# Expert outputs weighted and scattered to token order, and a last stage that reads them in order and adds on TensorE

## The chip, the cores and the metric

One core of a Trainium2 chip. The metric is device time of the whole program in microseconds, median over runs.

## The reference, cut to what matters

```python
x = x + _layernorm(attn_ref(_layernorm(x), ...))      # x: (32, 512, 256) float32; a Mamba scan and a block of layers
h = _layernorm(x)                                     # no gain, no bias
weights = router(h)                                   # per token: softmax over its 2 best of 8 experts
caw = weights * (cumsum(weights > 0, axis=0) <= 2048) # an expert takes its first 2048 tokens
out = relu(tokens @ first_linear.T) @ second_linear.T # per expert: 256 -> 512 -> 256
final = zeros.at[index].add(out * vals)               # each token: weighted sum of its experts' rows
x = x + _layernorm(final)
```

There are 16384 tokens and 8 experts of 2048 slots. A token that finds its experts full gets rows of zeros.

## The kernel before

`build` runs three phases, each a block of its own in which all five engines have their own program, with semaphores between them.

`attention_phase` (L109 to 1165) goes over 32 sequences of 512 tokens. A scan of 32 steps per sequence (`scan`) carries three interleaved streams of other work: `pre` for the next sequence, `post` and `late` for those behind. Each is a generator that yields slot numbers (three slots per scan step), which fixes the order by hand on each engine. On SP, `load_rows` (L351 to 358) brings B and C rows for the step two ahead, 512 KiB each, into rings of two and four buffers. VectorE's drive (L960) reads the B rows. `late` writes x1 (the residual sum) to DRAM, routes the tokens, puts weights and slots aside in `w_all` and `idx_all`, and GpSimd scatters each normalised row of `tb` to its two slots in `expert_in` with eight indirect DMAs (L555). `expert_in` was cleared at the start by ScalarE's DMAs (L571).

`expert_phase` (L1168 to 1307) goes over 32 blocks of 512 slots, four to an expert. SP loads weights (L1213, 1215) and slots X (L1219), TensorE turns X, multiplies twice (L1246, 1256), ScalarE and VectorE share the relu, VectorE copies the output from PSUM to O (L1305), and ScalarE stores O in slot order to `expert_out`. X, XT, I and O have two buffers.

`combine_phase` (L1310 to 1470) goes over 32 sequences with G = 4 buffer sets. VectorE clears two row tiles and copies indices (L1433 to 1435), GpSimd gathers rows for 4 tiles and 2 choices with eight indirect DMAs (L1388), ScalarE multiplies the first choice by its weight (L1403), VectorE adds the second (L1444) and takes statistics (L1449, 1454), ScalarE computes the power with two table functions (L1410, 1412) and normalises (L1417), VectorE adds x1 (L1467), SP stores. `turns` writes each engine's parts out in order: a part `(back, part)` handles the sequence `back` places behind.

## Time and profile before

| what | value |
|---|---|
| median of 3 runs (lowest, highest) | 7221.53 us (7217.19, 7222.52) |
| the profiled execution: time, span | 7217.93 us, 7216.2 us |
| busy: TensorE, VectorE, ScalarE, GpSimd | 5483.0, 5886.2, 3552.3, 4301.8 us |
| DMA: packets, MB, mean GB/s | 492087, 1297.78, 180 |
[...]

Busy is the time in which an engine had an instruction at work. The profile is of one execution. Lines are those of the kernel before. TensorE's fp32 product of 512 columns is recorded as two records. [...]

### The profile page before, as it was taken

What the parts mean: (1) busy time and instruction counts of PE and PEld (TensorE: products, weight loads), DVE (VectorE), ACT (ScalarE), POOL (GpSimd) and SP (SyncE); (2) the same over time, 40 slices, a digit from 0 to 9 for tenths busy, and PEclk for the clock granted to TensorE, in tenths of its full rate; (3) what the DMA queues carried; (4) which work ended last, traced back from release to release, by engine and by line L of the source; (5) the groups of instructions that cost most, each with busy time, mean ns of one, the idle gap of its engine ahead of it and who ended that gap; (6) DMA issues with size and microseconds to landing.
All of it is one profiled execution on the core that took longest, in us unless ns stands there. A gap on an engine that the chain in (4) does not pass through costs nothing. (4 is left out here: it accounts for less than half of the span.)

```text
span 7216.2 us, 70913 instructions
## 1 busy us (share of the span) xinstructions
PE 5483.0 (76%) x16640; PEld 2999.0 (42%) x16640; DVE 5886.2 (82%) x7907; ACT 3552.3 (49%) x5338; POOL 4301.8 (60%) x2865
## 2 busy tenths in 40 slices
PE   4788778888887888878788888888887888599700
PEld 1344444444444444444444444444444444466400
DVE  5999999999999999989999999999999998211255
ACT  3555555555555555555555555555555554111156
POOL 3666666666666666666666666666666666200176
PEclk8899898889999988898988889989989988699855
DMA  7656556655655555555555555555555555022253
GB/s 262 215 193 197 192 198 200 202 195 195 203 203 188 194 194 191 195 189 194 193 190 189 193 191 200 193 192 189 196 194 184 187 188 194 11 91 87 78 160 94
DMA packets 492087, 1297.78 MB, mean 180 GB/s; under 512 B 59311, under 2 KB 216625, under 8 KB 490561
## 3 DMA queue, kind: packets, MB, share of 16 engines
q1 hardware_dynamic: 440960, 1219.82, 50.7%
q10 hardware_dynamic: 26048, 38.95, 1.6%
q0 software_dynamic: 24576, 33.72, 1.5%
q8 instruction: 143, 2.34, 0.1%
q14 instruction: 360, 2.94, 0.1%
HBM read 1206.19 MB, written 119.54 MB: 184 GB/s over the span
## 5 line engine op out<-in xcount | busy, mean ns | idle before, releaser
L480 POOL TENSOR_TENSOR st<-st,C_rows 128x1024 f32<-128x1024 f32 x1024 | 2470.6, 2415 | 1155.7 <-DVE st L988 1154.3
L787 PE MATMUL y<-st,ident 128*128 128x512 f32 x4096 | 2163.0, 663 | 472.2 <-POOL st L480 426.5
L988 DVE TENSOR_TENSOR_SCAN st<-dA,drive 128x1024 f32<-128x1024 f32 x1024 | 2338.7, 2284 | 177.2 <-ACT dA L642 85.2
L642 ACT ACTIVATE dA<-delta,a_neg 128x511 f32<-128x511 f32 x2048 | 1382.3, 713 | 2155.2 <-DVE st L988 2146.7
L787 PEld LDWEIGHTS y<-st,ident 128*128 128x128 f32 x4096 | 830.3, 212 | 1520.0 <-issue 899.1
L960 DVE TENSOR_TENSOR drive<-du,B_rows 128x1024 f32<-128x1024 f32 x1024 | 1259.5, 1230 | 101.3 <-DVE du L955 18.2
L761 PE MATMUL pre_bank<-e_abs,in_w 128*128 128x512 f32 x1024 | 601.6, 718 | 178.2 <-DVE u L926 161.9
L1388 POOL DMA_INDIRECT rows<-expert_out,idx_c x256 | 266.3, 1040 | 621.5 <-DVE idx_c L1435 551.4
L555 POOL DMA_INDIRECT expert_in<-tb,idx x256 | 259.8, 1015 | 367.0 <-DVE idx_all L1163 306.0
L741 PE MATMUL post_bank<-d_w,gT 128*128 128x256 f32 x2048 | 467.0, 385 | 12.4 <-issue 11.6
L741 PEld LDWEIGHTS post_bank<-d_w,gT 128*128 128x128 f32 x2048 | 394.3, 193 | 119.9 <-issue 67.7
L761 PEld LDWEIGHTS pre_bank<-e_abs,in_w 128*128 128x128 f32 x1024 | 211.4, 219 | 445.6 <-issue 209.7
L926 DVE SCALAR_TENSOR_TENSOR u<-pre_bank,conv_w,u 128x511 f32<-128x511 f32 (+2 forms) x384 | 285.3, 743 | 22.6 <-ACT u L598 13.6
L642 ACT ACT_TABLE_LOAD x217 | 278.4, 1283 | 3.8
L741 PE MATMUL post_bank<-q_w,F 128*128 128x256 f32 x512 | 184.3, 538 | 121.2 <-ACT F L664 121.2
L937 DVE TENSOR_SCALAR rest<-e_abs 128x1024 f32<-128x1024 f32 x64 | 233.6, 3650 | 25.5 <-ACT e_abs L623 19.4
L858 PE MATMUL post_bank<-F,d_w 128*128 128x512 f32 x512 | 236.0, 604 | 20.6 <-ACT F L695 20.5
L468 POOL TENSOR_TENSOR rest<-e_abs,rest 128x1024 f32<-128x1024 f32 x64 | 179.2, 2800 | 107.9 <-DVE rest L937 107.9
L1246 PE MATMUL bank<-XT,w 128*128 128x512 f32 x512 | 229.9, 603 | 10.1 <-ACT XT L1273 10.1
L1305 DVE COPY O<-bank 128x512 f32<-128x512 f32 x64 | 41.2, 686 | 234.5 <-PE bank L1256 234.5
L1256 PE MATMUL bank<-w,I 128*128 128x256 f32 x1024 | 228.6, 381 | 3.3 <-issue 3.3
L858 PE MATMUL pre_bank<-F,d_w 128*128 128x512 f32 x512 | 230.2, 592 | 0.0
(190 smaller groups left out, 8027.8 us busy)
## 6 DMA issues: line engine op xcount, KB each, us to landing
B_rows<-bc_rows SPq DMA_DIRECT2D x1024, 512.0 KB
C_rows<-bc_rows SPq DMA_DIRECT2D x1024, 512.0 KB
xin<-in_x SPq DMA_DIRECT2D x32, 512.0 KB, 7.3
expert_in<-gT ACTq DMA_DIRECT2D x8, 2048.0 KB, 27.2
xn_rows<-xin SPq DMA_DIRECT2D x32, 512.0 KB, 6.2
h<-xn_rows SPq DMA_DIRECT2D x32, 512.0 KB, 6.5
x_res<-in_x SPq DMA_DIRECT2D x32, 512.0 KB, 3.6
x_rows<-x_res SPq DMA_DIRECT2D x32, 512.0 KB, 3.2
```

Of the source, the lines that this page charges most:

```text
L480: pool.tensor_tensor(tile[:, :, :], tile[:, :, :], bc[1][k % ROWS[1]][:, :, :], ALU.mult)\
L555: pool.indirect_dma_start(out=xe_dram, out_offset=bass.IndirectOffsetOnAxis(ap=idx[:, tile, choice:choice + 1], axis=0), in_=tb[:, tile, : ...
L642: return act.activation(dA[k % 2][:, j, 1:L], delta[par][:, c, 1:L], ACT.Exp, scale=a_neg[:, c, n:n + 1])
L741: last = pe.matmul(banks[tile // 2][:, (tile % 2) * D:(tile % 2 + 1) * D], srcT[:, c, tile * P:(tile + 1) * P], w[:, c, :], start=c == 0, ...
L761: last = pe.matmul(RB[m % 2][:, :], in_w[:, c, m * P:(m + 1) * P], xT[:, c, :], start=c == 0, stop=c == KD - 1)
L787: last = pe.matmul(Y[:, :], ident[:, :], st[k % RING][:, j, :], start=pair == 0 and j == 0, stop=pair == CU - 1 and j == 1)
L858: last = pe.matmul(FB[j % 4][:, :], d1_w[:, c, j * P:(j + 1) * P], F[:, c, :], start=c == 0, stop=c == KD - 1)
L926: dve.scalar_tensor_tensor(late, RB[c % 2][:, 0:L - 1 - j], conv_w[:, c, 2 - j:3 - j], late, ALU.mult, ALU.add).then_inc(pre_dve.did(f"con ...
L937: dve.tensor_scalar(rest[:, :, :], e_abs[:, c:c + 2, :], 1.0, 1.0, ALU.add, ALU.subtract)\
L960: dve.tensor_tensor(DR[:, :, :], DU[:, :].unsqueeze(1).to_broadcast([P, 2, L]), bc[0][k % ROWS[0]][:, :, :], ALU.mult).then_inc(scan_in.di ...
L988: dve.tensor_tensor_scan(st[k % RING][:, :, :].rearrange("p a l -> p (a l)"), dA[k % 2][:, :, :].rearrange("p a l -> p (a l)"), DR[:, :, : ...
L1388: pool.indirect_dma_start(out=rows[n][c][:, tile, :], out_offset=None, in_=ye_dram, in_offset=bass.IndirectOffsetOnAxis(ap=idx_c[n][:, til ...
```

## The change

Rows of `expert_in` become 264 floats wide: behind the 256 features stand the token's two weights, its two expert numbers and its own number, all kept in `tb_wide`; `w_all` and `idx_all` go. In the expert stage VectorE finds out which choice of the token this expert is, and from it the slot's weight and a destination row, `choice * 16384 + token`. The output is multiplied by the weight as it leaves PSUM, and GpSimd scatters it with four indirect DMAs per block into `rank_rows`, which holds 2 x 16384 rows in token order. Unused slots have an index out of bounds and are not written. `rank_rows` is cleared by one 1 MiB DMA per sequence on SP during attention. One sequence of x1 is loaded behind each block's X into `x1_all`, which holds all 32 (128 KiB per partition), four tokens to a partition. The last stage loads both choices' rows of a sequence in one DMA, adds them in PSUM by four products with the identity, takes statistics on VectorE from PSUM, the power on GpSimd, normalises on ScalarE in PSUM, adds x1 on VectorE and stores from `x1_all`.

The diff, cut; of the last stage only the new lines are shown:

```diff
@@ -84,24 +84,27 @@
     xn_v = [rows.rearrange("(t p) d -> p t d", p=P) for rows in xn_dram]
     x1_dram = nc.dram_tensor("x1_rows", (S, L, D), F32, kind="Internal").ap()
     x1_v = x1_dram.rearrange("s (t p) d -> s p t d", p=P)
-    xe_dram = nc.dram_tensor("expert_in", (NSLOT, D), F32, kind="Internal").ap()
-    ye_dram = nc.dram_tensor("expert_out", (NSLOT, D), F32, kind="Internal").ap()
-    xe_zero_v = xe_dram.rearrange("(a p r) d -> a p (r d)", p=P, r=16)
+    x1_wide_v = x1_dram.rearrange("s (p t) d -> s p t d", p=P)
+    out_wide_v = t["out"].rearrange("s (p t) d -> s p t d", p=P)
+    DW = D + 8
+    xe_dram = nc.dram_tensor("expert_in", (NSLOT, DW), F32, kind="Internal").ap()
+    xe_zero_v = xe_dram.rearrange("n d -> (n d)").rearrange("(a p r) -> a p r", p=P, r=12 * D)
     xe_v = xe_dram.rearrange("(n t p) d -> n p t d", t=TB, p=P)
-    ye_v = ye_dram.rearrange("(n t p) d -> n p t d", t=TB, p=P)
+    yr_dram = nc.dram_tensor("rank_rows", (2 * NTOK, D), F32, kind="Internal").ap()
+    yr_zero_v = yr_dram.rearrange("(s p r) d -> s p (r d)", s=S, p=P)
+    yr_v = yr_dram.rearrange("(c s p t) d -> s p c t d", c=2, s=S, p=P)
     with ExitStack() as whole:
         def sem(name):
             return whole.enter_context(nc.semaphore(name))
-        idx_all = whole.enter_context(nc.sbuf_tensor("idx_all", [P, S * TT, 2], U32))
-        w_all = whole.enter_context(nc.sbuf_tensor("w_all", [P, S * TT, 2], F32))
         ident = whole.enter_context(nc.sbuf_tensor("ident", [P, P], F32))
         ones = whole.enter_context(nc.sbuf_tensor("ones", [P, P], F32))
-        eps5 = whole.enter_context(nc.sbuf_tensor("eps5", [P, 1], F32))
         attention_phase(nc, t, dict(locals()), sem)
+        x1_all = whole.enter_context(nc.sbuf_tensor("x1_all", [P, S, TT, D], F32))
+        x1_loaded = sem("x1_loaded")
         expert_phase(nc, t, dict(locals()), sem)
         combine_phase(nc, t, dict(locals()), sem)
...
@@ -195,7 +197,13 @@
         F = sb("F", [P, KD, L])
         gT = sb("gT", [P, KF, L])
         h = sb("h", [P, TT, D])
-        tb = sb("tb", [P, TT, D])
+        tb_wide = sb("tb", [P, TT, DW])
+        tb = tb_wide[:, :, 0:D]
+        wts = tb_wide[:, :, D:D + 2]
+        top_f = tb_wide[:, :, D + 2:D + 4]
+        token = tb_wide[:, :, D + 4]
...
@@ -371,6 +379,10 @@
                 sp.wait_ge(*post_dve.at("h_sum", b - 2))
...
                 sp.dma_start(xn_v[par], xin[:, :, :]).then_inc(xn_stored, 16)
+                yield 44
+                zero_row = zeros[:, :].unsqueeze(1).to_broadcast([P, 2 * TT * D // zeros.shape[1], zeros.shape[1]])
+                sp.dma_start(yr_zero_v[b].rearrange("p (a r) -> p a r", r=zeros.shape[1]), zero_row)\
+                    .then_inc(rank_rows_zeroed, 16)
                 yield 50
                 sp.wait_ge(*pre_act.at("xd", b))
                 sp.dma_start(bc_dram[par], xd[R:NX, :]).then_inc(xd_stored, 16)
...
@@ -421,7 +434,10 @@
+            pool.memset(zeros[:, :], 0.0).then_inc(consts, 1)
+            pool.iota(next_token[:, :], pattern=[[P, TT]], base=-int(FAR), channel_multiplier=1,
+                      allow_small_or_imprecise_dtypes=True).then_inc(consts, 1)
+            pool.memset(tb_wide[:, :, D:DW], 0.0).then_inc(consts, 1)
...
@@ -554,7 +570,7 @@
                     tile, choice = divmod(n, 2)
                     pool.indirect_dma_start(
                         out=xe_dram, out_offset=bass.IndirectOffsetOnAxis(ap=idx[:, tile, choice:choice + 1], axis=0),
-                        in_=tb[:, tile, :], in_offset=None, bounds_check=NSLOT - 1, oob_is_err=False)\
+                        in_=tb_wide[:, tile, :], in_offset=None, bounds_check=NSLOT - 1, oob_is_err=False)\
...
@@ -568,8 +584,8 @@
                     act.dma_start(dst, src).then_inc(post_weights_in, 16)
             act.wait_ge(zero_tile, 1)
             for a in range(xe_zero_v.shape[0]):
-                act.dma_start(xe_zero_v[a], gT_flat).then_inc(zeroed, 16)
-            act.wait_ge(consts, 13)
+                act.dma_start(xe_zero_v[a], gT_flat[:, 0:xe_zero_v.shape[2]]).then_inc(zeroed, 16)
+            act.wait_ge(consts, 15)
             act.wait_ge(pre_weights_in, 16 * len(PRE_IN))
...
@@ -1132,7 +1148,10 @@
                 dve.wait_ge(*late_dve.at("oh1_pos", b))
                 dve.tensor_tensor(asg[:, :, :], oh[0][:, :, :], oh[1][:, :, :], ALU.add)\
                     .then_inc(late_dve.did("asg"), 1)
-                dve.tensor_copy(w_all[:, bass.ds(b * TT, TT), :], wts[:, :, :]).then_inc(late_dve.did("w_all"), 1)
+                dve.tensor_copy(token, next_token[:, :]).then_inc(late_dve.did("token"), 1)
+                dve.wait_ge(*late_dve.at("token", b))
+                dve.tensor_scalar(next_token[:, :], next_token[:, :], float(L), None, ALU.add)\
+                    .then_inc(late_dve.did("next_token"), 1)
...
@@ -1159,8 +1178,6 @@
                         .then_inc(late_dve.did(f"slot{i}"), 1)
                 dve.wait_ge(*late_dve.at("slot1", b))
                 dve.tensor_scalar(idx[:, :, :], slot_f[:, :, :], FAR, None, ALU.add).then_inc(late_dve.did("idx"), 1)
-                dve.wait_ge(*late_dve.at("idx", b))
-                dve.tensor_copy(idx_all[:, bass.ds(b * TT, TT), :], idx[:, :, :]).then_inc(late_dve.did("idx_all"), 1)
             all_sequences(dve, pre, scan, post, late)
...
@@ -1194,10 +1221,22 @@
+        e_meta = Steps(sem("e_meta"), [f"{name}{n}" for n in range(NB) for name in
+                                       (("mine", "w_mine", "w_slot", "dest", "dest_i")
+                                        + (("expert",) if n % QB == QB - 1 else ()))])
+        expert_set = sem("expert_set")
+        carried_pool_e = sem("carried_pool_e")
+        XL = S // (NE // 2 * NB)
+        assert XL * (NE // 2) * NB == S
+        def before_meta(n, i):
+            return e_meta.at(f"dest{n - 2}", i) if n >= 2 else e_meta.at(f"dest{NB + n - 2}", i - 1)
...
@@ -1216,7 +1255,13 @@
                             .then_inc(w_loaded[e], 16)
                     sp.wait_ge(*before(e_turn, n, 2, i))
...
+                    sp.wait_ge(*before_meta(n, i))
...
                     sp.dma_start(X[n % 2][:, :, :], xe_v[i * NB + n]).then_inc(slots_loaded[n % 2], 16)
+                    for part in range(XL):
+                        at = (i * NB + n) * XL + part
+                        sp.dma_start(x1_all[:, bass.ds(at, 1), :, :], x1_wide_v[bass.ds(at, 1)]
+                                     .rearrange("s p t d -> p s t d")).then_inc(x1_loaded, 16)
         @block.tensor
         def _(pe):
...
@@ -1282,15 +1325,56 @@
                             .then_inc(e_relu_act.did(n * KE // 2 + m // 2), 1)
                     if n + 1 < NB:
                         copy_turned(n + 1)
-                    act.wait_ge(*e_out.at(n, i))
-                    act.dma_start(ye_v[i * NB + n], O[n % 2][:, :, :]).then_inc(stored[n % 2], 16)
-            for half in range(2):
-                act.wait_ge(stored[half], 16 * (NE // 2) * (NB // 2) + 16)
+        @block.gpsimd
+        def _(pool):
+            e_sent.credit(pool)
+            with pool.Fori(0, NE // 2) as i:
+                for n in range(NB):
+                    pool.wait_ge(*e_out.at(n, i))
...
+                    pool.wait_ge(*e_meta.at(f"dest_i{n}", i))
...
+                    for tile in range(TB):
+                        pool.indirect_dma_start(
+                            out=yr_dram, in_=O[n % 2][:, tile, :], in_offset=None,
+                            out_offset=bass.IndirectOffsetOnAxis(ap=dest_i[n % 2][:, tile:tile + 1], axis=0),
+                            bounds_check=2 * NTOK - 1, oob_is_err=False).then_inc(stored, 16)
+                    pool.wait_ge(stored, 16 * TB * NB * i + 16 * TB * (n + 1))
+                    pool.sem_inc(e_sent.did(n), 1)
         @block.vector
         def _(dve):
-            for steps in (e_relu_dve, e_out):
+            for steps in (e_relu_dve, e_out, e_meta):
                 steps.credit(dve)
+            dve.memset(expert[:, :], 0.0).then_inc(expert_set, 1)
+            dve.wait_ge(expert_set, 1)
+            def slots_meta(n, i):
+                meta = X[n % 2]
+                dve.wait_ge(slots_loaded[n % 2], 16 * (NB // 2) * i + 16 * (n // 2 + 1))
...
+                if n % QB == 0:
+                    dve.wait_ge(*(e_meta.at(f"expert{n - 1}", i) if n else e_meta.at(f"expert{NB - 1}", i - 1)))
+                dve.tensor_scalar(mine[:, :, :], meta[:, :, D + 2:D + 4], expert[:, 0:1], None, ALU.is_equal)\
+                    .then_inc(e_meta.did(f"mine{n}"), 1)
+                dve.wait_ge(*e_meta.at(f"mine{n}", i))
+                dve.tensor_tensor(w_mine[:, :, :], mine[:, :, :], meta[:, :, D:D + 2], ALU.mult)\
+                    .then_inc(e_meta.did(f"w_mine{n}"), 1)
+                dve.wait_ge(*e_meta.at(f"w_mine{n}", i))
+                dve.tensor_reduce(w_slot[:, :], w_mine[:, :, :], AX_X, ALU.add)\
+                    .then_inc(e_meta.did(f"w_slot{n}"), 1)
+                dve.scalar_tensor_tensor(dest[:, :], mine[:, :, 1], float(NTOK), meta[:, :, D + 4],
+                                         ALU.mult, ALU.add).then_inc(e_meta.did(f"dest{n}"), 1)
+                dve.wait_ge(*e_meta.at(f"dest{n}", i))
+                dve.wait_ge(*before(e_sent, n, 2, i))
+                dve.tensor_scalar(dest_i[n % 2][:, :], dest[:, :], FAR, None, ALU.add)\
+                    .then_inc(e_meta.did(f"dest_i{n}"), 1)
+                if n % QB == QB - 1:
+                    dve.tensor_scalar(expert[:, :], expert[:, :], 1.0, None, ALU.add)\
+                        .then_inc(e_meta.did(f"expert{n}"), 1)
             with dve.Fori(0, NE // 2) as i:
...
@@ -1298,47 +1382,45 @@
                         dve.wait_ge(*e_mm1.at(n * KE + m, i))
                         dve.tensor_scalar(I[n % 2][:, m, :], MB[m][:, 0:BLK], 0.0, None, ALU.max)\
                             .then_inc(e_relu_dve.did(n * KE // 2 + m // 2), 1)
+                    slots_meta(n, i)
                     dve.wait_ge(*e_mm2.at(n, i))
-                    dve.wait_ge(stored[n % 2], 16 * (NB // 2) * i + 16 * (n // 2 + 1))
-                    for tile in range(0, TB, 2):
-                        last = dve.tensor_copy(O[n % 2][:, tile:tile + 2, :],
-                                               OB[tile // 2][:, :].rearrange("p (a d) -> p a d", a=2))
+                    dve.wait_ge(*e_meta.at(f"w_slot{n}", i))
+                    for tile in range(TB):
+                        last = dve.tensor_scalar(O[n % 2][:, tile, :],
+                                                 OB[tile // 2][:, (tile % 2) * D:(tile % 2 + 1) * D],
+                                                 w_slot[:, tile:tile + 1], None, ALU.mult)
                     last.then_inc(e_out.did(n), 1)
 def combine_phase(nc, t, env, sem):
...
@@ -1360,114 +1442,101 @@
+            sp.wait_ge(x1_loaded, 16 * S)
...
+                sp.wait_ge(*c_sum.at(n, i - 1))
+                sp.dma_start(rows[n][:, :, :, :], yr_v[G * i + n]).then_inc(rows_loaded[n], 16)
+                sp.dma_start(out_wide_v[bass.ds(G * i + n, 1)].rearrange("s p t d -> p s t d"),
+                             x1_all[:, bass.ds(G * i + n, 1), :, :]).then_inc(out_stored, 16)
+            sp.wait_ge(out_stored, 16 * S)
+        @block.tensor
+        def _(pe):
+            c_sum.credit(pe)
+            def add(n, i):
+                pe.wait_ge(rows_loaded[n], 16 * (i + 1))
+                pe.wait_ge(*c_out.at(n, i - 1))
+                for half in range(TT // 2):
+                    for c in range(2):
+                        last = pe.matmul(total[n][:, 2 * half:2 * half + 2, :].rearrange("p t d -> p (t d)"), ident[:, :],
+                                         rows[n][:, c, 2 * half:2 * half + 2, :].rearrange("p t d -> p (t d)"),
+                                         start=c == 0, stop=c == 1)
+                last.then_inc(c_sum.did(n), 1)
+            turns(pe, ((0, add),))
+        @block.vector
+        def _(dve):
+            for steps in (c_stats, c_out):
+                steps.credit(dve)
+            dve.wait_ge(x1_loaded, 16 * S)
+            def stats(n, i):
+                dve.wait_ge(*c_sum.at(n, i))
+                for tile in range(TT):
+                    last = dve.bn_stats(stat[n][:, tile, :], total[n][:, tile, :])
+                last.then_inc(c_stats.did(f"stats{n}"), 1)
+                dve.wait_ge(*c_stats.at(f"stats{n}", i))
...
+                for tile in range(TT):
+                    last = dve.bn_aggr(mv[n][:, tile, :], stat[n][:, tile, :])
+                last.then_inc(c_stats.did(f"aggr{n}"), 1)
+            def add(n, i):
+                dve.wait_ge(*c_normed.at(n, i))
+                x1 = x1_all[:, bass.ds(G * i + n, 1), :, :].rearrange("p s t d -> p (s t d)")
+                dve.tensor_tensor(x1, total[n][:, :, :].rearrange("p t d -> p (t d)"), x1, ALU.add)\
+                    .then_inc(c_out.did(n), 1)
+            turns(dve, ((2, add), (0, stats)))
+            c_shift.credit(pool)
+            pool.memset(minus_half[:, :], -0.5).then_inc(c_const, 1)
+            pool.wait_ge(c_const, 1)
+            def scale_and_shift(n, i):
+                pool.wait_ge(*c_stats.at(f"aggr{n}", i))
...
+                pool.wait_ge(*c_normed.at(n, i - 1))
...
+                pool.tensor_scalar(shift[n][:, :], mv[n][:, :, 0], -1.0, None, ALU.mult).then_inc(c_shift.did(f"m{n}"), 1)
+                pool.tensor_scalar(r[n][:, :], mv[n][:, :, 1], LN_EPS, None, ALU.add).then_inc(c_shift.did(f"v{n}"), 1)
+                pool.wait_ge(*c_shift.at(f"v{n}", i))
+                pool.tensor_tensor(r[n][:, :], r[n][:, :], minus_half[:, :], ALU.pow).then_inc(c_shift.did(f"r{n}"), 1)
+                pool.wait_ge(*c_shift.at(f"r{n}", i))
+                pool.tensor_tensor(shift[n][:, :], shift[n][:, :], r[n][:, :], ALU.mult)\
+                    .then_inc(c_shift.did(f"shift{n}"), 1)
+            turns(pool, ((0, scale_and_shift),))
+            c_normed.credit(act)
+                act.wait_ge(*c_shift.at(f"shift{n}", i))
+                for tile in range(TT):
+                    last = act.activation(total[n][:, tile, :], total[n][:, tile, :], ACT.Identity,
+            turns(act, ((0, normalise),))
```

## Rows read from the trace of the kernel before

**Rows 1.** Stretches of the span: start:end, us, busy time (instructions) per engine, clock, DMA share, GB/s.

```profile
0.00:6311.88 6311.88, 5001.22 (x14848) 2677.77 (x14848) 5590.25 (x7203) 3263.09 (x4826) 4035.53 (x2609) 0.89 0.57 191
6311.88:6819.79 507.91, 481.81 (x1792) 321.26 (x1792) 85.48 (x128) 72.57 (x128) 0.00 (x0) 0.98 0.25 83
6819.79:7216.20 396.41, 0.00 (x0) 0.00 (x0) 210.42 (x576) 216.67 (x384) 266.30 (x256) 0.50 0.42 127
```

**Rows 2.** Groups of the combine stage: count | busy us, mean ns | idle before, releaser.

```profile
L1388 POOL DMA_INDIRECT rows<-expert_out,idx_c x256 | 266.3, 1040 | 621.5 <-DVE idx_c L1435 551.4 <-issue 70.1
...
L1444 DVE SCALAR_TENSOR_TENSOR rows<-rows,w_c,rows 128x256 f32<-128x256 f32 x128 | 53.4, 480 | 18.6 <-ACT rows L1403 17.5 <-issue 1.0
L1449 DVE BATCH_NORM_STATS2 c_stat<-rows 128x6 f32<-128x256 f32 x128 | 45.0, 414 | 16.6 <-remote 9.1 <-issue 5.3 <-DVE rows L1444 1.3
...
L1467 DVE TENSOR_TENSOR x<-x,rows 128x1024 f32<-128x1024 f32 x32 | 39.3, 1228 | 110.7 <-ACT rows L1417 89.7 <-issue 21.0
```

**Rows 3.** Timeline at the combine's start: start us, us, engine, instruction, [idle before].

```profile
6819.79 1.48 SPq L1369 DMA_DIRECT2D x<-x_rows  x3
...
6829.76 0.99 POOL L1388 DMA_INDIRECT rows<-expert_out,idx_c  x1 [0.30 <-issue]
```

**Rows 4.** Timeline of the program's start, ScalarE's clearing DMAs.

```profile
28.22 5.46 ACTq L571 DMA_DIRECT2D expert_in<-gT  x8
```

**Rows 5.** Timeline around slot 44 of one sequence, SP's queue and VectorE.

```profile
2991.68 0.34 SPq L357 DMA_DIRECT2D C_rows<-bc_rows  x1
2999.16 0.32 SPq L357 DMA_DIRECT2D B_rows<-bc_rows  x1
...
3007.63 1.23 DVE L960 TENSOR_TENSOR drive<-du,B_rows 128x1024 f32<-128x1024 f32 x1
```

**Rows 6.** The 32 loads of X (L1219, 512 KiB), from issue to landing.

```profile
DMA to landing us min/median/max: 3.7/3.9/6.4
```

**Rows 7.** Single microseconds of attention: TensorE busy (count), granted clock, DMA share, GB/s.

```profile
3047.00:3048.00 1.00, 0.00 (x0) 1.00 1.02 369
3048.00:3049.00 1.00, 0.00 (x0) 0.61 1.01 336
...
3054.00:3055.00 1.00, 1.00 (x2) 0.50 0.00 0
...
3056.00:3057.00 1.00, 1.00 (x7) 1.00 1.04 373
```

**Rows 8.** Timeline of the last expert block.

```profile
6799.61 6.60 PE L1246 MATMUL bank<-XT,w 128*128 128x512 f32 x15
...
6807.04 7.15 PE L1256 MATMUL bank<-w,I 128*128 128x256 f32 x32 [0.83 <-issue]
6814.23 1.29 DVE L1305 COPY O<-bank 128x512 f32<-128x512 f32 x2 [7.28 <-PE bank L1256]
6815.75 0.38 ACTq L1286 DMA_DIRECT2D expert_out<-O  x1
```

**Rows 9.** Timeline of one layer norm at the end of the attention stage.

```profile
6271.95 0.38 DVE L911 BATCH_NORM_AGGREGATE mv_late<-stat_late 128x2 f32<-128x6 f32 x4
...
6274.50 2.07 ACT L580 ACTIVATE tb<-tb,shift_late,r_late 128x256 f32<-128x256 f32 x4 [25.92 <-POOL shift_late L457]
```

**Rows 10.** Timeline of the border from attention to the experts.

```profile
6307.42 0.97 POOL L555 DMA_INDIRECT expert_in<-tb,idx  x1 [0.31 <-issue]
6311.88 0.40 SPq L1213 DMA_DIRECT2D w<-in_e_w  x1
...
6318.94 1.96 PE L1231 MATMUL bank<-ident,X 128*128 128x128 f32 x8 [23.08 <-DMA X<-expert_in]
```

**Rows 11.** Timeline: fp32 products of 512 columns at either clock.

```profile
45.10 6.77 PE L761 MATMUL pre_bank<-e_abs,in_w 128*128 128x512 f32 x8 [1.16 <-ACT e_abs L592]
...
3002.64 1.96 PE L787 MATMUL y<-st,ident 128*128 128x512 f32 x4
```

**Rows 12.** Timeline: the last add of the program.

```profile
7211.21 1.23 DVE L1467 TENSOR_TENSOR x<-x,rows 128x1024 f32<-128x1024 f32 x1 [2.14 <-ACT rows L1417]
```

158 lines of the change are left out of this document (50 added, 108 removed).

## The prediction

> **What bounds the kernel now.** I read the stretches first, then the groups of the last stage, the order of time around each border, and last the clock. The program is three stages one behind the other [rows 1]: attention and routing to 6311.88 us, the experts for 507.91 us, the combine for 396.41 us. In the first, VectorE is busy 5590 of 6312 us and is the limit. In the second, TensorE is busy 482 of 508 us at clock 0.98. In the third TensorE does nothing and the DMA share is 0.42; look there at the GpSimd row: 256 gathers [rows 2], one issued every 0.99 + 0.30 = 1.30 us [rows 3]. Eight for each sequence are 10.4 us, times 32 sequences 333 us of the 396; the rest is the fill, the drain and waits for the cleared buffers. ScalarE (two table loads a sequence) and VectorE lie beside it. So the combine is set by GpSimd's issuing, 12.4 us a sequence, and that is what the change removes.
>
> **The sum's base.** The profiled execution took 7217.9 us (span 7216.2), 3.6 us under the median of the runs shown, 7221.5; I work against 7217.9 and predict with no correction. Stages one and two and the combine are summed separately, and the new combine replaces 396.4 us.
>
> **Attention.** The two small copies per sequence (`w_all`, `idx_all`) go and two small ones (`token`, `next_token`) come, on VectorE both: nil. Scattered rows grow from 1024 to 1056 bytes, with the same eight issues: nil. SP now waits for GpSimd's constants before its first load of x; these are a handful of short fills done while SP issues weight loads: nil. ScalarE issues 11 instead of 8 clearing DMAs ahead of its first activation, on which the start hangs: eight took 5.46 us [rows 4], so three more are 2.0 us; rows are a quarter shorter, bounds 0 and 2.0, I take 1.4. New on SP's queue is one 1 MiB clearing write per sequence, at slot 44 of `pre`, which is behind the C load issued at 2991.68 and before the B load issued at 2999.16 in this sequence [rows 5]. The queue is to do 1.5 MiB in that 7.5 us gap. Behind it waits the B load, used by the drive at 3007.63, 8.5 us after its issue, where a 512 KiB load lands in 3.9 us [rows 6]. That leaves 4.6 us of cover, and the write moves at about 373 GB/s [rows 7] in 2.8 us. So nil; bounds 0 and 1 us per sequence (32 us), taken 0 because both covers would have to go.
>
> **Experts.** The path is TensorE: from the first product of a block's first layer at 6799.61 to the end of its second layer at 6814.19 lie 14.6 us, and it is busy all through [rows 8]. The X load waits also for VectorE's `dest` of the block two back, about half a block later than now; there remain more than 10 us until its transposes, against a landing of 3.9 us at the median and 6.4 at most [rows 6]. The 512 KiB load of x1 goes behind it in SP's queue. VectorE gets five or six tiny operations (four aggregates together cost 0.38 [rows 9]), under 2 us, between the second relu and the end of the second product, where it idled 7.28 us [rows 8]. The output becomes four scaled copies of 256 columns in place of two of 512. The nearest rows are the 1.29 us of now and four scalar_tensor_tensor at 480 ns [rows 2], 1.9 us at most; TensorE needs the banks one first product (7 us) later. GpSimd gets four scatters (5.2 us) and the wait for their landing, about 9 us for a block, and the buffer is wanted two blocks later. Nothing of this is on the path except behind the last block. There, before, 4.0 us lie between ScalarE's store and the first load of the combine [rows 3, 8]. After: 0.4 us more for the output, 0.2 us, four issues at 1.30, and then what lay between the end of the last scatter of the attention stage and the first load of the experts, 6311.88 - 6308.39 = 3.5 us [rows 10]. That is 9.3 us less 0.5 that both have, so 4.8 us are added (bounds 3 and 7). Where all this idle time is gone, an expert block pays at most about 2 us, 64 us in all; the cover is several times the cost, so I take 0.
>
> Before the combine that makes +6.2 us.
>
> **The new combine.** Per sequence: one 1 MiB load, four fp32 products with the identity (both choices summed in PSUM), bn_stats, GpSimd's power, ScalarE's normalise, one add, one 512 KiB store. It clears nothing, gathers nothing and loads no tables, and x1 lies in SBUF already. Throughput first: VectorE 1.41 + 0.38 + 1.23 = 3.0 us [rows 2, 9], GpSimd 2.0, ScalarE 2.1, 1.5 MiB at 373 GB/s 4.2 us, TensorE 8 records. Eight records took 6.77 us at the lower clock; four took 1.96 at the higher, so eight about 3.7 [rows 11].
>
> But the order of issue makes a ring. On SP `store(n-3)` stands before `load(n)`, so load n is issued only when the add of n-3 is done. On VectorE the add of n stands behind the statistics of n+1. From sum n+1 to the end of the add of n: statistics 1.41 + 0.15 + 0.38 = 1.95 (SBUF prices; PSUM could be up to 0.2 more), add 1.25, hops 0.1: 3.3 us. Sum n's own way to its add (statistics 1.95, GpSimd's four steps until ScalarE starts 2.17, normalise 2.07 [rows 9]: 6.2 us) is shorter than that, as long as the period is above 4.3. From there to sum n+3: hop 0.1, store and load, hop 0.1, products. For store and load I use two rows. Two weight loads and X, 1.5 MiB in one burst, took from 6311.88 to 6318.94, 7.06 us [rows 10], and one 512 KiB load alone takes 3.9 [rows 6]. So 3.16 us is for 1 MiB (332 GB/s) and 2.3 us is fixed. The new transfers have pieces of 4 KiB, as the B and C loads, in whose busy microseconds 369 and 373 GB/s stand [rows 7]: 4.2 + 2.3 = 6.5 us. So sum n+3 lies 3.3 + 6.7 + products after sum n+1, and the period T is half of 10.0 + products: 6.85 us at the higher clock, 8.4 at the lower.
>
> The products' clock: the granted clock was still 1.00 in the idle microsecond from 3047, fell to 0.61 in the next, was 0.50 in the microsecond from 3054, the last of nearly four busy ones, and 1.00 from 3056 [rows 7]. A burst of 3.7 us in a period of 7 leaves gaps of over 3 us; a burst of 6.8 leaves 1.6. I expect bursts of both kinds in turn, mean 5.25 us, T = 7.6.
>
> Fill: load 0 lands at 5.1 us, sum 0 at 12.0 (1.2 GHz), sum 1 at 17.3, add 0 done at 20.6, sum 3 at 32.6. Then 28 periods of 7.6, 213 us, then sum 31's way to its add, 6.2 + 1.3, and from the last add to the span's end 3.8 [rows 12]: 256.7 us. The sum is 7217.9 - 396.4 + 6.2 + 256.7 = **7084 us**.
>
> [...]
>
> **The rivals.** [...] (b) The ring doesn't bind, and transfers set the pace, because the landing time overlaps better than I think: T = 5.3, combine about 192, **7020 us**. For it: 4.2 us is the transfer time and three loads are in flight. Against it: the written order on SP and VectorE. (c) The covers in the first two stages are thinner, 1 us per sequence or block in one of them and 1 to 2 in the other: 7084 + 32 to 96, about **7140 us**. For it: VectorE is 89% busy in attention, so any stall there counts fully. (d) Slower than before: the clearing write holds the B loads back. It costs something once it takes over 8.3 us (3.7 of gap left by the C load, 4.6 of cover), and makes the kernel slower when each of 32 sequences stalls for over 4.2 us. At 5 us that is **7244 us**; the write would have to run at 79 GB/s, where the row shows 373. (e) The change doesn't do what it says: the combine stays at 12 us a sequence since something else as long as the gathers stands behind them: about 7215. Nothing in rows 2 is that long, since ScalarE's two table loads go too.
>
> **How the numbers follow.** Forecast 0.50 (7061 to 7109, T from 6.85 to 8.4); (a) 0.13; (b) 0.20; (c) 0.12; (d) 0.03; (e) 0.02. The prediction is 7084. The range reaches down to (b), 7020, and up to a part of (c), 7125, and leaves out about half of (c), (d), (e) and the faster end of (b). A measurement of this kernel can tell some 0.2% (14 us) from no change, and all of the forecast, (a), (b) and (c) lie beyond that: faster 0.95, same 0.02, slower 0.03.
>
> **What would show it.** The combine should be 235 to 282 us with sums 7 to 8.5 us apart, and TensorE waiting for the loaded rows, each load issued right after an add three back. VectorE should wait for the sums before its statistics. If the sums lie 5 us apart, (b). [...] The expert stage should be 508 + 5 us, the attention stage 6312 + 1.4; more there is (c) or (d), seen as VectorE's drive waiting for B_rows. A combine whose busy records of statistics or normalise are much longer from PSUM than from SBUF would make my 3.3 us wrong.

## The result and the profile after

| | before | after |
|---|---|---|
| device time, median (lowest to highest) | 7221.15 us (7217.19 to 7222.52, 4 runs) | 7121.35 us (7114.18 to 7126.48, 4 runs) |
| ratio | | 0.9862, interval 0.9845 to 0.9879 |
| profiled execution, time and span | 7217.9, 7216.2 us | 7119.3, 7117.5 us |
| attention and routing | 6311.88 us | 6339.18 us, +27.3 (forecast +1.4) |
| experts | 507.91 us | 506.73 us, -1.2 (forecast +4.8) |
| combine | 396.41 us | 271.59 us, -124.8 (forecast -139.7) |

The change takes 99.8 us off the median; the forecast was 137 (7221 to 7084). It is faster, by 1.4% and clear of its interval, and inside the range given, 7020 to 7125, near its upper end. By the profiles it is 98.7 us, and the three stage lines of the table add up to that. This is the view of stretches for the kernel after, as [rows 1]: start:end, us, then busy time (instructions) of PE, PEld, DVE, ACT and POOL, granted clock, DMA share, GB/s.

```profile
0.00:6339.18 6339.18, 5002.93 (x14848) 2691.31 (x14848) 5598.24 (x7204) 3263.38 (x4826) 4050.88 (x2611) 0.89 0.58 196
6339.18:6845.91 506.73, 480.12 (x1792) 320.56 (x1792) 120.47 (x360) 72.59 (x128) 124.86 (x129) 0.98 0.35 117
6845.91:7117.50 271.59, 153.62 (x256) 61.34 (x256) 95.91 (x288) 60.98 (x128) 54.68 (x128) 0.75 0.53 185
```

GpSimd's 266.30 us of gathers in the combine have become 54.68 us, and its 128 scatters stand in the expert stage, where it was at 0.00 before. No engine is busy for even 60% of the new combine. From the page of the kernel after, a group (count, busy us, mean ns, idle before with its releaser), and two DMA lines (count, KB each, us to landing):

```profile
L1472 PE MATMUL total<-rows,ident 128*128 128x512 f32 x256 | 153.6, 763 | 118.4 <-DMA rows<-rank_rows 118.2
...
rank_rows<-zeros SPq DMA_DIRECT2D x32, 1024.0 KB, 7.8
rows<-rank_rows SPq DMA_DIRECT2D x32, 1024.0 KB, 6.7
```

The 118.2 us in the first line is what the combine now waits for: loads. They land in 6.7 us at the median; they are issued late. One round in time order (start us, us, engine, instruction, idle before with its releaser; consecutive instructions of the same kind are drawn together):

```profile
6889.59 9.60 PE L1472 MATMUL total<-rows,ident 128*128 128x512 f32 x16 [6.71 <-DMA rows<-rank_rows]
...
6895.74 1.42 DVE L1489 BATCH_NORM_STATS2 c_stat<-total 128x6 f32<-128x256 f32 x4 [8.74 <-PE total L1472]
...
6897.61 1.19 DVE L1501 TENSOR_TENSOR x_all<-total,x_all 128x1024 f32 x1
...
6899.03 0.36 SPq L1456 DMA_DIRECT2D out<-x_all  x1
6899.23 1.42 DVE L1489 BATCH_NORM_STATS2 c_stat<-total 128x6 f32<-128x256 f32 x4 [0.43 <-PE total L1472]
6899.65 0.38 SPq L1451 DMA_DIRECT2D rows<-rank_rows  x1
...
6905.40 8.03 PE L1472 MATMUL total<-rows,ident 128*128 128x512 f32 x11 [6.21 <-DMA rows<-rank_rows]
...
6912.18 1.09 DVE L1489 BATCH_NORM_STATS2 c_stat<-total 128x6 f32<-128x256 f32 x3 [8.85 <-PE total L1472]
```

Read it as a ring. The sum that starts at 6889.59 frees VectorE's statistics at 6895.74; behind them in VectorE's order stands the add of the sequence before, done at 6898.80; it frees SP's store and, behind that, the next load, issued at 6899.65; its rows start TensorE at 6905.40. The sums come in pairs, 16.4 us apart (6895.74 to 6912.18). From load 3 at 6866.09 to load 31 at 7094.28 are 228.2 us for 28 periods, T = 8.15.

Single microseconds of that round (same columns as the stretches):

```profile
6887.00:6888.00 1.00, 0.00 (x0) 0.00 (x0) 0.01 (x1) 0.77 (x2) 0.20 (x1) 0.83 0.95 377
6890.00:6891.00 1.00, 1.00 (x2) 0.42 (x2) 0.00 (x0) 0.00 (x0) 0.00 (x0) 0.50 0.65 152
6894.00:6895.00 1.00, 1.00 (x3) 0.53 (x2) 0.00 (x0) 0.00 (x0) 0.00 (x0) 0.76 0.22 90
6896.00:6897.00 1.00, 1.00 (x4) 0.50 (x3) 1.00 (x4) 0.00 (x0) 0.00 (x0) 1.00 0.00 0
```

The first sum of the pair starts after 6.7 us of idleness, by the end of which the clock is 0.50. It takes 6.2 us (6889.59 to 6895.74), and the clock comes back in the last of it: 0.76 in the microsecond from 6894, 1.00 in the one from 6895. The second follows directly at clock 1.00 and takes 3.4 us. Over the stage the first sums of the 14 pairs from 6874.13 on took 5.2 to 6.8 us, 6.05 in the mean, and their starts lie 16.15 us apart in the mean. Each of the 14 starts at clock 0.50. The second sum of a pair has its rows already, or waits 1.2 us for them at the most, and takes 3.4 to 3.7 us.

The start of the program, where [rows 4] had eight DMAs in 5.46 us:

```profile
28.02 11.66 ACTq L587 DMA_DIRECT2D expert_in<-gT  x11
```

Eleven took 11.66 us: 6.2 more, where the forecast had 1.4 with an upper bound of 2.0.

The rest of attention's loss is in its loop. From the 336.69 us at which one store of `bc_rows` is issued to the last such of the loop, 5878.31, before took 5541.6 us; after (342.96 to 5909.27) took 5566.3: +24.7. The start had put +6.3 ahead of that, and the last stretch gives 3.7 back. The groups of the loop's window, 336 to 5900 us (count, busy us, mean ns, idle before), of the kernel before:

```profile
L555 POOL DMA_INDIRECT expert_in<-tb,idx x232 | 235.7, 1016 | 321.6 <-DVE idx_all L1163 266.4 <-issue 55.2
L1054 DVE TENSOR_SCALAR gcol<-post_bank,rg 128x2 f32<-128x2 f32 x30 | 6.6, 219 | 29.4 <-POOL rg L447 29.4
```

The same groups of the kernel after:

```profile
L571 POOL DMA_INDIRECT expert_in<-tb,idx x224 | 239.8, 1070 | 313.9 <-DVE idx L1180 252.0 <-issue 61.9
L1070 DVE TENSOR_SCALAR gcol<-post_bank,rg 128x2 f32<-128x2 f32 x29 | 6.3, 218 | 47.3 <-POOL rg L463 47.3
```

A scatter costs 54 ns more in the mean, and VectorE waits 18 us longer for GpSimd before `gcol`. One sequence shows which scatter it is, and nearly all others are like it. The timeline of the kernel before:

```profile
3000.34 0.17 DVE L1161 TENSOR_SCALAR idx<-slot_f 128x8 uint32<-128x8 f32 x1
...
3000.64 0.17 DVE L1163 COPY idx_all<-idx 128x8 uint32 x1
...
3002.82 0.98 POOL L555 DMA_INDIRECT expert_in<-tb,idx  x1 [0.30 <-issue]
3003.05 0.68 DVE L955 TENSOR_TENSOR du<-delta,u 128x512 f32<-128x512 f32 x1
...
3012.04 0.22 DVE L1054 TENSOR_SCALAR gcol<-post_bank,rg 128x2 f32<-128x2 f32 x1 [0.81 <-POOL rg L447]
```

The same place in the kernel after:

```profile
3017.79 0.17 DVE L1180 TENSOR_SCALAR idx<-slot_f 128x8 uint32<-128x8 f32 x1
...
3020.18 0.68 DVE L971 TENSOR_TENSOR du<-delta,u 128x512 f32<-128x512 f32 x1
...
3020.27 1.44 POOL L571 DMA_INDIRECT expert_in<-tb,idx  x1 [0.30 <-issue]
...
3029.95 0.22 DVE L1070 TENSOR_SCALAR gcol<-post_bank,rg 128x2 f32<-128x2 f32 x1 [1.58 <-POOL rg L463]
```

With the 0.17 us copy gone, VectorE reaches `du` 0.32 us sooner after `idx` (2.39 us against 2.71). Before, the second scatter started 0.23 us ahead of `du` and took 0.98 us; after, it starts 0.09 us behind `du` and takes 1.44. So it is in 28 of the loop's 29 sequences (in the other the second scatter comes later and is short in both kernels): before, the second scatter starts ahead of `du` in 27 and takes 0.97 or 0.98 us, and in the one where it starts 0.06 behind it takes 1.46; after, it starts 0.08 to 0.36 us behind `du` in each and takes 1.44 down to 1.17, so that it always ends some 1.52 us after `du` began. `gcol` waits for GpSimd's power, and comes 12.16 us after `idx` instead of 11.70: 0.46 us a sequence, some 14 us of the loop's 24.7.

In the expert stage, this is a loop's edge in the timeline of the kernel before:

```profile
6446.08 0.38 ACTq L1286 DMA_DIRECT2D expert_out<-O  x1
6447.05 1.07 ACT L1273 COPY XT<-bank 128x512 f32<-128x512 f32 x2 [11.80 <-issue]
...
6448.25 8.20 PE L1246 MATMUL bank<-XT,w 128*128 128x512 f32 x15 [3.08 <-ACT XT L1273]
```

And one in the kernel after:

```profile
6472.24 1.07 ACT L1316 COPY XT<-bank 128x512 f32<-128x512 f32 x2 [10.06 <-PE bank L1276]
...
6473.45 7.13 PE L1291 MATMUL bank<-XT,w 128*128 128x512 f32 x16 [1.34 <-ACT XT L1316]
```

Before, ScalarE had to issue the store of `expert_out` (and so wait for VectorE's output) ahead of the copy that TensorE waits for. With the store gone, TensorE waits 1.34 instead of 3.08 us. There are three such edges (3.08, 2.86 and 2.84 us before, 1.3 each after), which is 4.8 us. At this one the next sixteen records also took 8.63 us before and 7.13 after; at the other two they took 7.13 before already. This is read from the timelines; no run puts the store back. From the first transpose to the last product the stage took 488.8 us instead of 495.3.

### The profile page after: what moved, and what is told of

Same layout as the page of the kernel before. It is cut to its first block and busy times, and to the rows that moved or that the text cites. A ratio compares the mean times of both kernels' runs of the same rounds, so it can differ in the third digit from the quotient of the medians.

```text
span 7117.5 us, 71413 instructions
## 1 busy us (share of the span) xinstructions
PE 5636.7 (79%) x16896; PEld 3073.2 (43%) x16896; DVE 5814.6 (82%) x7852; ACT 3397.0 (48%) x5082; POOL 4230.4 (59%) x2868
## 5 line engine op out<-in xcount | busy, mean ns | idle before, releaser
L1339 POOL DMA_INDIRECT rank_rows<-O,dest_i x128 | 124.8, 975 | 382.1 <-issue 382.1
L1472 PE MATMUL total<-rows,ident 128*128 128x512 f32 x256 | 153.6, 763 | 118.4 <-DMA rows<-rank_rows 118.2
L1291 PE MATMUL bank<-XT,w 128*128 128x512 f32 x512 | 228.2, 599 | 5.3 <-ACT XT L1316 5.3
```

## The experiments

The attention stage ends with the first weight load of the experts; "border" below is its time (before 6311.88, after 6339.18). Each ratio is to the kernel before on the same chip. Chips differed: before had medians of 7191.9 us beside the first four, 7237.3 beside the next four and 7197.3 beside the last four. The gather stage took 396.4 us in the profile of the kernel before, but 373.2 and 375.4 us in the profiles of two variants that don't touch it (experiments three and ten), on other chips; why is not known. There the change is worth less: experiment two is the changed kernel with one write moved, and its ratio is 0.9904, 69 us, where the changed kernel itself had 0.9862. Where kernels stand beside each other I therefore go by the borders and the length of the combine.

**Is the clearing write the cause in attention?** First without it. The last stage reads x twice in place of the scattered rows.

```diff
-                yield 44
-                sp.dma_start(yr_zero_v[b]..., zero_row).then_inc(rank_rows_zeroed, 16)
 ...
-                sp.dma_start(rows[n][:, :, :, :], yr_v[G * i + n])
+                sp.dma_start(rows[n][:, :, :, :], x_rows.unsqueeze(1).to_broadcast([P, 2, TT, D]))
```

> The changed kernel without the 1 MiB clearing write per sequence; rank_rows is not cleared, and the last stage loads rows of x twice in its place (same transfer size, other data). Question: the attention stage of the changed kernel ends 27.3 us later than before, 6.2 of it at the start and 21 us gathered over 32 sequences. Theory A (the clearing write in flight beside the scatters and the B and C loads costs it): the first expert load comes 17 to 24 us earlier than 6339.2, the whole time is about 7101, and the idle time before VectorE's gcol (47 us against 27 before) falls back. Rival B (the wider rows of tb and the token copies cost it): the border stays within 5 us of 6339, the time at 7121.

Ratio 0.9879 (0.9864 to 0.9894), median 7107.1 us; the profiled execution, with a span of 7112.7, is the slowest of the four. Its border is at 6349.42, 10 us later than with the write, and the loop takes 5572.3 us. The loss isn't the clearing's. The added 10 us were expected by no theory. Some 4 of them are spread: the four profiles of experiments five to eight, whose attention stage is that of the changed kernel, have borders from 6338.73 to 6343.06. The rest is not explained.

**The write in another place of the same sequence.**

```diff
-                yield 44
 ...
+                yield 70
```

The three lines of the write move with it, behind the store of `bc_rows` at slot 50.

> The changed kernel with the clearing write at slot 70 of pre in place of 44, behind the last scatter (slot 53). Theory A1 (it costs because it runs beside the scatters, which GpSimd issues more slowly, and G's power waits behind them): the border between attention and experts comes 12 to 21 us earlier than 6339.2, time 7100 to 7109. A2 (1 MiB more per sequence costs wherever it stands): within 5 us of 6339, time 7116 to 7126. B (wide rows): no change either.

0.9904 (0.9889 to 0.9919), median 7122.9 us; the border is at 6340.40 and the loop takes 5566.3 us, as after. The place is of no account either.

**The write alone, in the kernel before**, with the tile of zeros that it reads and SP's wait for it.

```diff
 ...
+                sp.dma_start(yr_zero_v[b]..., zero_row).then_inc(rank_rows_zeroed, 16)
```

> The kernel before with the clearing write alone (1 MiB per sequence at slot 44 into a DRAM tensor that nobody reads). Theory A: 17 to 24 us slower than before, 7238 to 7245, all of it ahead of the expert stage. B: within 5 us of before, 7216 to 7226.

1.0001 (0.9992 to 1.001). Border 6315.42, which is 3.5 us later, scatters 1017 ns in the mean, the wait ahead of `gcol` 29.9 us in all. So 32 MiB of clearing beside the attention stage cost nothing clear of the noise, and the forecast's zero held.

**The eleven clearings of expert_in spread over the first scan**, so that nothing waits for their issue.

```diff
-            for a in range(xe_zero_v.shape[0]):
-                act.dma_start(xe_zero_v[a], ...).then_inc(zeroed, 16)
 ...
+                    if isinstance(b, int) and b == 0 and k < xe_zero_v.shape[0]:
+                        act.dma_start(xe_zero_v[k], ...).then_inc(zeroed, 16)
```

> The changed kernel with the 11 clearing DMAs of expert_in issued one by one in the first 11 steps of the first scan on ScalarE, and not ahead of its first activation. If ScalarE's issuing (11.7 us here, 5.5 before) stands on the path of the start, the whole program shifts by 10 to 12 us: 7109 to 7111. If the first loads of x or weights end later than I think, 0 to 5 us.

0.9921 (0.9906 to 0.9936), and the border went the wrong way, to 6356.70. The first store of `bc_rows` is 11 us earlier (64.73 against 75.57), but the one that stood at 342.96 is at 357.97. VectorE's waits between 70 and 350 us (us in total, times, longest), first with the clearings spread:

```profile
DVE drive L976 <- DMA B_rows<-bc_rows: 29.3, 10, 5.9
```

The same wait in the kernel after:

```profile
DVE drive L976 <- DMA B_rows<-bc_rows: 0.7, 1, 0.7
```

The 16.5 MiB of clearing now pass beside the first scan's loads, where VectorE is the limit, and the waits for those loads grow by 29 us, against the 11 us gained. It was expected 10 to 12 us faster than the kernel after; the border is 17.5 us later.

**The order on SP.** The load of n ahead of the store of n-3: the load of n now stands behind the add of n-4 in place of n-3, so the ring through the add holds one period more.

```diff
-            turns(sp, ((3, store), (0, load)))
+            turns(sp, ((0, load), (3, store)))
```

> The changed kernel with SP's two parts in the other order, load(n) ahead of store(n-3), so that a load is issued behind the add of four sequences back in place of three. Ring theory (period 8.15 us set by order of issue: half of 3.1 us from the first sum of a pair to an add, 6.6 to the landed rows, 6.5 for products at the lower clock): the ring now holds three periods, T = 16.3/3 = 5.4 us, or 4.7 if the clock stays up; the combine falls from 271.6 to 175 to 200 us, time 7025 to 7050. Rival (the transfers set the pace, 1.5 MiB in 8.15 us): no change, 7115 to 7126.

0.9725 (0.9709 to 0.9742), 7039.6 us. The combine takes 189.97 us, and from load 4 at 6868.99 to load 31 at 7015.60 T = 5.43 (the expectation of the last experiment has it as 5.24). View of stretches, as above:

```profile
6848.83:7038.80 189.97, 136.08 (x256) 54.58 (x256) 96.06 (x288) 60.89 (x128) 54.50 (x128) 0.84 0.75 265
```

This settles the ring: same instructions, same bytes, 82 us less.

**The order on VectorE.** The add of n-1 ahead of the statistics of n.

```diff
-            turns(dve, ((2, add), (0, stats)))
+            turns(dve, ((1, add), (0, stats)))
```

> The changed kernel with VectorE's add one place behind in place of two, so that the add of n no longer stands behind the statistics of n+1. Ring theory: the ring becomes 7.4 (statistics, power, normalise, add) + 6.6 + products over three periods: 17.5 to 20.5 us, T = 5.9 to 6.8, the combine 210 to 235 us, time 7060 to 7085. Rival (transfers set the pace): no change.

0.9817 (0.98 to 0.9833); the combine takes 255.2 us, a miss of 20 us at the least. The timeline shows what took the ring's place:

```profile
6881.59 1.22 DVE L1501 TENSOR_TENSOR x_all<-total,x_all 128x1024 f32<-128x1024 f32 x1 [4.21 <-ACT total L1535]
...
6882.73 1.42 DVE L1489 BATCH_NORM_STATS2 c_stat<-total 128x6 f32<-128x256 f32 x4
...
6886.94 1.90 ACT L1535 ACTIVATE total<-total,c_shift,c_r 128x256 f32<-128x256 f32 x4 [5.38 <-POOL c_shift L1523]
...
6889.03 1.22 DVE L1501 TENSOR_TENSOR x_all<-total,x_all 128x1024 f32 x1 [4.36 <-ACT total L1535]
```

VectorE's statistics, GpSimd's power, ScalarE's normalise and VectorE's add now follow one another within one period, 7.44 us. VectorE waits 110.0 us for ScalarE between 6875 and 7060. I had counted the shorter way to the add and not that it made a loop of its own.

**Both orders.**

```diff
-            turns(sp, ((3, store), (0, load)))
+            turns(sp, ((0, load), (3, store)))
-            turns(dve, ((2, add), (0, stats)))
+            turns(dve, ((1, add), (0, stats)))
```

> Both changes of order together (load ahead of store, add one place behind). Ring: 7.4 + 6.6 + products over four periods, 4.4 to 5.1 us, so that another limit takes over: TensorE's group at 3.4 to 4.7 us, or 1.5 MiB at 373 GB/s, 4.2 us. T = 4.4 to 5.2, the combine 165 to 190 us, time 7015 to 7040. Transfers set the pace at 8.15: no change.

0.982 (0.9804 to 0.9837); combine 254.4 us, as with VectorE's order alone. VectorE's loop binds whatever SP does. The 165 to 190 us expected are missed for the same cause as in the experiment before.

**The products.** The rows of the second choice are loaded and not added, four records instead of eight.

```diff
-                    for c in range(2):
-                        last = pe.matmul(total[n]..., start=c == 0, stop=c == 1)
+                    for c in range(1):
+                        last = pe.matmul(total[n]..., start=True, stop=True)
```

> The changed kernel with the products of the first choice only; the second choice's rows are loaded and not added. TensorE's group halves, from 3.4 us at the higher and 6.5 at the lower clock to 1.7 and 3.3. Ring theory with products on the ring at the lower clock: the pair's 16.3 us fall by 3.2, T = 6.5, the combine 225 us, time 7075. If the products on the ring ran at the higher clock, the pair would lose 1.7 and the combine 24 us: 7098. Transfers set the pace: no change.

0.9785 (0.9769 to 0.9802); combine 234.3 us. The starts of the first group of each pair lie 13.9 us apart in the mean (14 pairs from 6873.78 to 7068.31), T = 6.9. A pair was 16.15 by the same count, so it fell by 2.3, and the first group fell by as much, from 6.05 to 3.71 us. That is the ring with this group on it once. Whether the second group is off it this run can't say: it starts at the lower clock here too in most pairs (0.53 over the one from 6922.90 on, 0.50 over the one from 7047.45 on) and takes about 3.6 us, no less than with twice the records at the higher clock. That it is off the ring is read from the timeline after, where the load of each pair's first sum is issued behind the add that follows the other first sum's statistics. The 225 us expected took the cold group from 6.5 us to 3.3.

**The copy back in attention.**

```diff
                 dve.tensor_scalar(idx[:, :, :], slot_f[:, :, :], FAR, None, ALU.add)
+                dve.wait_ge(*late_dve.at("idx", b))
+                dve.tensor_copy(idx_all[:, bass.ds(b * TT, TT), :], idx[:, :, :])...
```

> The changed kernel with the small copy of idx behind idx put back (nobody reads it). Theory C: the attention stage became 25 us longer because without this copy (0.3 us on VectorE) the next scan, and with it the du product of VectorE, comes 0.3 us earlier against GpSimd's scatters; the second scatter then runs into du (1.44 us for it in place of 0.98), GpSimd's power for G comes 0.5 to 0.8 us later and gcol waits 1.6 us in place of 0.8. Then the copy takes the idle time before gcol back from 47 to 27 to 30 us, the mean scatter in the loop from 1070 to 1017 ns, and the whole time falls by 10 to 25 us, to 7096 to 7111 on the first chip, a ratio to before of 0.983 to 0.985. Rival B (the wider rows make the scatter itself slower): the scatter stays at 1070 ns and gcol at 47 us, the ratio at 0.986.

0.9871 (0.9856 to 0.9886), 7104.0 us. The time is in the band expected; the ratio, expected at 0.983 to 0.985, is not, and says little here, since the gather stage of the kernel before is some 21 us shorter on this chip. The border is at 6323.09, 16.1 us earlier, for 32 instructions more. Its groups of the loop are those of before:

```profile
L572 POOL DMA_INDIRECT expert_in<-tb,idx x230 | 234.1, 1018 | 326.2 <-DVE idx_all L1183 270.6 <-issue 55.5
L1071 DVE TENSOR_SCALAR gcol<-post_bank,rg 128x2 f32<-128x2 f32 x30 | 6.5, 218 | 28.5 <-POOL rg L464 28.5
```

The loop takes 5548.7 us, 17.6 of the 24.7 back. The 7.1 that stay are of the size of the spread: with this copy, the wide rows and the token copies the last two experiments have loops of 5542.1 and 5549.0 us, where the kernel before has 5541.6 and experiment three 5545.5. Without the copy the profiles of the changed kernel and of experiments one, two and four to eight have 5562.0 to 5572.3. So the wide rows cost a few microseconds at the most; alone they were not tried.

**The reverse in the kernel before:** the copy made later in the sequence.

```diff
+                yield 47
                 dve.wait_ge(*late_dve.at("idx", b))
                 dve.tensor_copy(idx_all...
```

> The kernel before with its idx_all copy moved three slots later, so that nothing stands between idx and the next scan, as in the changed kernel. Theory C: the mean scatter in the loop goes from 1016 to about 1070 ns, the idle time before gcol from 29 to 45 us, and the kernel becomes 10 to 25 us slower than before, 0.15 to 0.35%. Rival B (wider rows): no change, within 5 us.

1.0016 (1.0007 to 1.0025). Border 6326.57, +14.7, and a scatter 1068 ns (groups of the loop):

```profile
L555 POOL DMA_INDIRECT expert_in<-tb,idx x229 | 244.5, 1068 | 320.6 <-DVE idx L1161 256.9 <-issue 58.9 <-DVE ssg L1051 4.5
L1054 DVE TENSOR_SCALAR gcol<-post_bank,rg 128x2 f32<-128x2 f32 x30 | 5.8, 195 | 5.7 <-POOL rg L447 5.7
```

The longer scatter is as expected: the second of each sequence starts 0.07 to 0.37 us behind `du` and takes up to 1.45 us. The size of the loss is as expected too, but the way is not: the wait ahead of `gcol`, expected at 45 us, is 5.7. The timeline shows where the time goes:

```profile
3012.09 2.38 POOL L480 TENSOR_TENSOR st<-st,C_rows 128x1024 f32<-128x1024 f32 x1
3012.58 1.93 DVE L1164 COPY idx_all<-idx 128x8 uint32 x1
...
3014.43 0.15 DVE L1051 TENSOR_REDUCE ssg<-post_bank 128x1 f32<-128x4 f32 x1
```

The moved copy took 0.17 us in its old place. Here it starts beside GpSimd's `st` and takes 1.93 us, at the median too, until `st` is done. That is 49 us more in the loop (54.3 against 5.0), and VectorE, late by that, no longer waits for GpSimd. So this run shows again what makes the second scatter dear, but its loss of 16.7 us in the loop (5558.3 against 5541.6) is not evidence that the dear scatter costs that much; for that the copy put back in the changed kernel stands alone.

**All that helped together:** the load first, the copy back, and nine clearings of expert_in (eight of 16 rows' width and a small one) instead of eleven.

```diff
-    xe_zero_v = ....rearrange("(a p r) -> a p r", p=P, r=12 * D)
+    xe_zero_v = [view[a] for view in
+                 (xe_flat[0:whole_zero].rearrange("(a p r) -> a p r", p=P, r=16 * D),
 ...
```

The other two edits are those shown above.

> The changed kernel with three edits: load ahead of store on SP, the idx copy put back, and expert_in cleared by 8 DMAs of 2 MiB and a small one (9 issues) in place of 11 of 1.5 MiB. From the load-first kernel (7040, ratio 0.973): 5 us less at the start if the issues take 0.7 us each as before (0 if it is the bytes waiting), 10 to 25 us less in attention if theory C holds. 7010 to 7030 by C and the start, ratio 0.969 to 0.971; 7035 to 7041 if neither.

0.9749 (0.9734 to 0.9764), 7011.5 us. The time is in the band expected, the ratio (0.969 to 0.971) again is not. The nine take 7.03 us, the border is at 6312.46, the combine takes 186.9 us. The start in its timeline:

```profile
27.93 7.03 ACTq L591 DMA_DIRECT2D expert_in<-gT  x9
```

**The store on ScalarE's queue**, on top of that, so that no load stands behind a store.

```diff
-            turns(sp, ((0, load), (3, store)))
+            turns(sp, ((0, load),))
-            turns(act, ((0, normalise),))
+            turns(act, ((0, normalise), (3, store)))
 ...
```

> The last kernel, but with the stores of the last stage issued on ScalarE behind its normalise, three sequences back, so that SP's loads wait for nothing but a free buffer. With load first the period was 5.24 us. If the ring through the add still set it, T falls to 4.4 to 4.8 us (1.5 MiB at 373 GB/s is 4.2) and the combine by 12 to 24 us against the last kernel. If the transfers already set it at 5.2 us (300 GB/s), no change.

0.9675 (0.966 to 0.969), 6963.3 us (6961.2 to 6966.8): the fastest here, its profiled span 152 us under that of the kernel after, on another chip. The combine is 139.3 us, 47.6 less than in the last kernel, twice what I expected at the most. Two stretches of its combine:

```profile
6850.00:6900.00 50.00, 49.65 (x114) 20.74 (x113) 38.73 (x123) 25.88 (x55) 22.45 (x53) 1.00 1.01 400
6900.00:6940.00 40.00, 39.31 (x86) 15.25 (x86) 31.76 (x95) 19.87 (x42) 18.55 (x43) 1.00 1.03 420
```

TensorE is busy for 49.65 of 50 us at clock 1.00, and the DMA share is 1. I had expected a period of 4.4 to 4.8 us from 1.5 MiB at 373 GB/s; 400 to 420 GB/s passed, and the period came down to 3.7 (32 sums from 6830.99 to 6949.96). From 6890 to 6940 TensorE idles for 0.86 us in all and the clock stays at 1.00, and its products, 3.7 us a sequence (14.78 us for the four from 6905.09 on), are as long as the period.

## Why the prediction was right, and where it was off

**What bounded the kernel** held: GpSimd's 333 us of gather issues were the combine [rows 2, 3], and without them it is 124.8 us shorter.

**The combine's ring** was the likeliest case, at a forecast T of 7.6, and is the one that came, at 8.15; experiments five and seven show it. By its terms, in the mean of 14 pairs and in brackets for the round above: sum to the end of the add 3.3 us (6895.74 to 6898.80, 3.1; forecast 3.3, from SBUF prices [rows 2, 9]; from PSUM the statistics cost 1.42 us and the add 1.2, so nothing was added); store and load with both hops 6.8 us (6898.80 to 6905.40, 6.6; forecast 6.7 [rows 6, 7, 10]); products 6.05 us (6905.40 to 6912.18, 6.8, the longest of all). The mis-sized term is this last: I took the mean of a cold and a warm group, 5.25. I had foreseen bursts of both kinds in turn, but the ring links every second sum, and all those it links start cold, at clock 0.50. With 6.05 the pair is 16.15 and T 8.1. That is 28 x 0.5 = 14 us, against 14.9 measured. The fill (load 3 at 20.2 us; forecast add 0 at 20.6) and the end agree. A mean over two states may only be used when the path passes both.

Some terms of that sum stand in no run. The 1.2 GHz that the prediction puts beside its first sum is one of them: the traces give the clock as a share, 0.50 at the start of each first sum and 0.75 over the stage; over the whole span it was 0.875 before and 0.890 after. That the eight records of 6.77 us in [rows 11] ran at the lower clock isn't shown either, since the view of stretches gives 1.00 for 45 to 52 us of the kernel before. What stands at 0.50 there is four such records in 3.78 us, from 3051.24 on. And the up to 0.2 us more that it allowed for PSUM did not come: 1.42 us for the statistics (6895.74), where four from SBUF had taken 1.41 in the kernel before (6270.40).

**The experts** came out at -1.2 where +4.8 was forecast. The addition at the end was right in kind: 5.60 us from the last product to the combine before, 11.06 after, so 5.5 against 4.8 [rows 3, 8, 10]. What I missed is the gain of 6.5 us at the loop's edges. The prediction looked at one block [rows 8] and gave the removed store of `expert_out` no term at all; at the edges it stood ahead of the copy that TensorE waits for.

**The start** is a mis-sized term: 6.2 us for three more clearings, bound at 2.0. I took 0.68 us each from eight [rows 4]. Nine, of which one was small, took 7.03 and 6.15 us; eleven took 11.5 to 13.3 for the same 16.5 MiB. The price of one more was not the mean of the first eight. Why the last ones are dear was not tried.

**The attention loop** is the step that failed, though the time stayed inside the range: "two small copies go and two come: nil". 24.7 us came from it, 17.6 of them by the removal of a copy, which putting it back shows. What cost the time wasn't an instruction but, as I read it, the place of `du` against the second scatter, which moved by 0.3 us. That the scatter is slowed when `du` starts first is in the start times of 28 sequences in each of four profiles (before, after, nine and ten). That it reaches VectorE through `gcol` is argued from the wait, 47.3 us after and 28.5 with the copy back. Up to 7 us of the loop, and some 6 us of the kernel without clearing, are open.

**The clearing write**: nil was right. Rival (d) was rightly thought small: the write alone in the kernel before gave 1.0001.

**The rivals.** (b) needed the order on SP changed: with the load first the combine took 190 us, which is the 192 and the T of 5.3 that (b) gave, but for the cause I had named for it, transfers setting the pace, the last kernel speaks against it, since there the same bytes pass in 139 us. (a), all groups of products at the lower clock, has T = 8.4 and a combine of 282 us, nearer to the measured 271.6 than the forecast's 256.7, but for the wrong reason: the second sums ran at clock 1.00, in 3.4 to 3.7 us, and the ring didn't feel them. (c) said 1 us a sequence for thinner covers; 0.8 came, through none of the covers that I had named. The time lies 3.6 us inside the range's upper end, which was drawn for (c), and that it held is in part luck. Not (e): the combine changed as said.

## What to carry to other kernels

When a stage's engines are all under 60% busy, write out the ring of waits through the in-order queues and count each link at the state it is in when the ring passes it; then look for a store standing ahead of a load, since moving one line here was worth 80 us and a second queue 48 more. Before an operation is shifted, even by a removal of 0.2 us, look at what runs beside it on the neighbouring engine. After every such change compare stage borders, or a loss in one stage hides behind a gain in another.
